# Preparing the feed-forward's first rows some blocks ahead, and multiplying its first chunk in the pause of the local attention's last block

## The chip, the cores and the metric

One core of one Trainium2 chip runs the whole program in one launch. The core has five engines with an instruction queue each: TensorE (PE in the profile, PEld for its weight loads), VectorE (DVE), ScalarE (ACT), GpSimd (POOL) and SyncE (SP), which here only issues DMAs. They meet through semaphores. The metric is the device time of the launch in microseconds; less is better.

## The reference

Four sequences of 1024 rows of 256 numbers go through a layernorm. A causal attention of 16 heads gives `s`; a stack of two layers, each a local attention and a gated feed-forward, gives the gate `g`; the result is `x + s * silu(g)`. The part that matters is one layer:

```python
h = shift_token(x); qkv = h @ wqkv                  # second half of the columns from the row before
q, k = rotary_xpos(l2norm(q) * qs, l2norm(k) * ksc) # 8 heads of 64
x = x + local_attention(q, k, v) @ wo               # window of 128: own block and the one before
h = shift_token(x)
h = (h - h.mean(-1)) / sqrt(h.var(-1) + 1e-5) * lg + lb
a, g = split(h @ w1 + b1, 2)                        # 2 x 682 columns
x = x + (a * gelu(g)) @ w2 + b2
```

## The kernel before, in words

The program runs project, causal attention, and then for each of two layers `phase_window` (local attention) and `phase_feed` (feed-forward). Each phase is a block of its own: all engines meet at its end, and no engine begins the next one before. Every engine's order is written out by hand.

`phase_window` goes over 32 blocks of 128 rows (`NW`; `w` is the block). In step `w` PE runs `project(w+2)` (18 matmuls of 512 columns with the weights `qkv_hi`, `qkv_lo`), `attend(w)` (turn the normalised probabilities `pn` in four parts, turn keys and queries of block `w+1`, then `values`), `turn_h(w+3)`, `score(w+1)` and `output(w)`. DVE runs `normalise(w)` in two halves, `unit(w+1)`, `copy_last`, `cosines` and `sum_squares` of `w+2`, `lo_out`, the `maxima` of `w+1` and `residual(w)`, which writes x1. ACT runs the eight `exps(w)`, which wait for the maxima, and the copies out of PSUM. POOL runs the rotation (`rope`) for `w+2`. SP stores x1 and loads the rows of block `w+4`. A product of full precision is made of three: high by high, high by low, low by high part.

`phase_feed` goes over 8 groups of 512 rows (`SUPERS`; 4 tiles each) and 6 chunks of hidden columns, the last one short. For each chunk PE does `up` (12 matmuls of 512 columns, 6 for the short one) into one of two pairs of PSUM banks (`pH`), ACT does the Gelu and the high part, DVE the product with the gate (`gated`), POOL the low part. A chunk waits for the `gated` of the chunk two before it. In the middle of the first group's chunks PE turns group 1 (`turn(1, 1)`), which needs `hn` of group 1. ACT splits w2 (`w2_hi`, L1627) behind the first chunk's high part.

The attention phase already works for the feed-forward of its layer. SP's `start_feed` in step 28 loads the small constants, w1 (into `qkv_st`, free by then) and, last, two groups of rows. ACT's `feed_weights` makes the high parts of w1 in three parts, the first behind the exps of block 30, two more in step 30; they overwrite `qkv_hi`, so they wait for the last projection. DVE's `feed_split` makes the low parts in steps 30 and 31. For group 0, DVE computes moments at the end of step 30 (`feed_moments`), POOL the deviation, DVE normalises in step 31 (`feed_normalise`), PE turns the rows behind the values of block 31 into banks 0 and 1 of `pS`, the scores' tensor, ACT scales them and makes the high part (`feed_rows`), and DVE makes the low part behind the last residual (`feed_lo`). In step 30 and 31 there is no projection left, so PE has a pause ahead of `attend` (called the pause of block 30 or 31 below).

## Time and profile before

| | us |
|---|---|
| median of 3 runs | 1919.55 (1918.88 to 1920.72) |
| the profiled execution | 1915.72 |
| its span | 1913.6 |
| PE, DVE, ACT, POOL busy | 1816.2, 1462.9, 1211.3, 1000.4 |
| layer 0: attention about 613 to 1047, feed-forward 1047 to 1247 | |
| layer 1: attention 1247 to 1678, feed-forward from 1678 | |

The span is the time from the first to the last instruction of the profiled execution; its time has 2.1 us more around it. PE is busy for 95% of the span, so what counts is where it waits, and at which clock it runs. The busy times of the others say little by themselves: in each stretch one asks what ended the wait of the engine that sets the pace.

### The profile page before, as it was taken

The page shows a single profiled execution, that of the slowest core. Times are in us where ns is not written, and L with a number is a line of the kernel's source. Part 1 is how long each engine was busy: PE and PEld are TensorE (multiplying, and loading weights), DVE is VectorE, ACT ScalarE, POOL GpSimd, SP SyncE. Part 2 cuts the span into 40 slices and gives each one's busy share as a digit, 9 for nine tenths or more (in the row PEclk, how much of TensorE's full clock was granted, in tenths as well). Part 3 has the DMA queues.
Part 4 walks back from the last instruction along what each step waited for, and adds up shares of the span by engine and source line. Part 5 has one row for each costly group of instructions (what it writes and reads, how often), then busy time and mean ns, then how long its engine had stood idle before and what let it go on. Part 6 is the DMA issues. An engine that isn't in the chain of part 4 may idle for free. (4 is left out here: it accounts for less than half of the span.)

```text
span 1913.6 us, 37326 instructions
## 1 busy us (share of the span) xinstructions
PE 1816.2 (95%) x12768; PEld 1298.9 (68%) x12768; DVE 1462.9 (76%) x4115; ACT 1211.3 (63%) x2537; POOL 1000.4 (52%) x807
## 2 busy tenths in 40 slices
PE   7979999999998899999997999989999999889998
PEld 6723333333333788888886888868888888778998
DVE  6678888888882899999997544379999999854543
ACT  4606666666666777777776544358777877655553
POOL 5532223223122778777873444367787778444343
PEclk9959999999999999999998999999999999899999
DMA  8983646455430000100022331100000100242222
GB/s 283 306 145 48 79 57 86 65 73 76 60 48 23 15 29 22 29 29 29 22 58 56 104 114 52 34 30 29 29 24 27 29 29 25 65 126 76 79 78 88
DMA packets 142456, 128.10 MB, mean 67 GB/s; under 512 B 31106, under 2 KB 124734, under 8 KB 142014
## 3 DMA queue, kind: packets, MB, share of 16 engines
q1 hardware_dynamic: 141214, 124.68, 28.4%
q8 instruction: 104, 1.70, 0.4%
q10 hardware_dynamic: 1056, 1.05, 0.2%
q14 instruction: 82, 0.67, 0.1%
HBM read 83.46 MB, written 41.96 MB: 66 GB/s over the span
## 5 line engine op out<-in xcount | busy, mean ns | idle before, releaser
L675 ACT ACTIVATE ca_pr<-ca_pS 128x1024 f32<-128x1024 f32 (+3 forms) x384 | 296.5, 811 | 204.9 <-PE ca_pS L589 163.9
L503 POOL TENSOR_SCALAR_AFFINE_SELECT ca_pr<-ca_pr 128x256 f32<-128x256 f32 x256 | 103.2, 406 | 367.5 <-ACT ca_pr L675 363.1
L704 DVE CUSTOM_DVE_ANT_0 ca_masked<-ca_pR,ca_later 128x256 f32<-128x256 f32 (+3 forms) x512 | 235.6, 485 | 44.7 <-PE ca_pR L565 41.6
L565 PE MATMUL ca_pR<-ca_ks,ca_qs 96*128 96x512 bf16 (+3 forms) x768 | 219.5, 344 | 6.8 <-DVEq L760 3.1
L589 PE MATMUL ca_pS<-ca_qs,ca_ks 98*128 98x512 bf16 (+3 forms) x768 | 183.8, 330 | 12.4 <-issue 6.7
L708 DVE TENSOR_REDUCE ca_mx<-ca_pR 128x1 f32<-128x512 f32 x256 | 175.7, 686 | 25.0 <-PE ca_pR L565 23.2
L565 PEld LDWEIGHTS ca_pR<-ca_ks,ca_qs 96*128 96x128 bf16 x768 | 70.5, 97 | 161.7 <-DVE ca_mx L704 90.1
L941 POOL TENSOR_TENSOR wb_tsn<-wb_qk,base 128x512 f32<-128x512 f32 x62 | 136.5, 2223 | 69.0 <-DVE wb_pn L1156 67.6
L941 POOL TENSOR_TENSOR w_tsn<-w_qk,base 128x512 f32<-128x512 f32 x62 | 136.5, 2222 | 69.0 <-DVE w_pn L1156 67.6
L610 PE MATMUL ca_pO<-ca_pr,ca_va 128*32 128x512 f32 (+3 forms) x1536 | 164.5, 500 | 1.6 <-POOL ca_pr L503 0.8
L1012 ACT ACTIVATE w_pe<-w_sm,w_nmax 128x256 f32<-128x256 f32 (+1 forms) x256 | 123.3, 483 | 67.0 <-DVE w_nmax L1146 66.8
L1012 ACT ACTIVATE wb_pe<-wb_sm,wb_nmax 128x256 f32<-128x256 f32 (+1 forms) x256 | 123.2, 483 | 66.3 <-DVE wb_nmax L1146 66.3
L589 PEld LDWEIGHTS ca_pS<-ca_qs,ca_ks 98*128 98x128 bf16 x768 | 62.2, 98 | 114.5 <-ACT ca_pr L675 66.8
L1156 DVE TENSOR_SCALAR wb_pn<-wb_pe,wb_rsum 128x256 f32<-128x256 f32 (+1 forms) x256 | 97.1, 441 | 2.3
L1156 DVE TENSOR_SCALAR w_pn<-w_pe,w_rsum 128x256 f32<-128x256 f32 (+1 forms) x256 | 96.6, 439 | 2.3
L1146 DVE CUSTOM_DVE_ANT_0 w_sm<-w_pS,masks 128x256 f32<-128x256 f32 (+1 forms) x256 | 88.7, 403 | 9.5 <-PE w_pS L1380 9.3
L1146 DVE CUSTOM_DVE_ANT_0 wb_sm<-wb_pS,masks 128x256 f32<-128x256 f32 (+1 forms) x256 | 88.6, 403 | 9.0 <-PE wb_pS L1380 9.0
L949 POOL TENSOR_TENSOR wb_rs<-wb_ssc,mhalf 128x16 f32<-128x16 f32 x32 | 94.0, 2938 | 2.7
L949 POOL TENSOR_TENSOR w_rs<-w_ssc,mhalf 128x16 f32<-128x16 f32 x32 | 93.9, 2934 | 2.7
L1561 POOL TENSOR_TENSOR f_alo<-f_af,f_ahi 128x512 fp32r<-128x512 f32 x40 | 53.3, 1332 | 54.1 <-ACT f_ahi L1624 54.1
L1561 POOL TENSOR_TENSOR fb_alo<-fb_af,fb_ahi 128x512 fp32r<-128x512 f32 x40 | 53.2, 1330 | 52.9 <-ACT fb_ahi L1624 52.9
L1704 DVE SCALAR_TENSOR_TENSOR fb_af<-fb_pH,fb_b1a,fb_gl 128x512 f32<-128x512 f32 x40 | 30.0, 750 | 63.0 <-ACT fb_gl L1621 58.4
(297 smaller groups left out, 5396.3 us busy)
## 6 DMA issues: line engine op xcount, KB each, us to landing
QKP<-p_parts SPq DMA_DIRECT2D x32, 384.0 KB, 3.6
ca_qs<-QKP SPq DMA_DIRECT2D x96, 128.0 KB, 6.5
ca_ks<-QKP SPq DMA_DIRECT2D x96, 128.0 KB, 7.2
w_xt<-X SPq DMA_DIRECT2D x64, 128.0 KB, 2.2
X<-w_x SPq DMA_DIRECT2D x64, 128.0 KB, 1.7
f_hh<-X SPq DMA_DIRECT2D x32, 256.0 KB, 6.0
X<-p_xn SPq DMA_DIRECT2D x8, 512.0 KB, 4.8
VA<-p_vst SPq DMA_DIRECT2D x8, 512.0 KB, 4.7
```

The source lines that it names most:

```text
L565: pe.matmul(bank[:, 0:w], qs[0:SHIFT_ROW, u, h, i * P:(i + 1) * P], ks[0:SHIFT_ROW, u, h, k0:k0 + w], start=True, stop=True).then_inc(ring ...
L589: ins = pe.matmul(pS[:, pair, hh, 0:w], ks[:, u, h, j * P:(j + 1) * P], qs[:, u, h, q0:q0 + w], start=True, stop=True)
L610: ins = pe.matmul(pO[h * VW:(h + 1) * VW, o:o + w], va[:, u, j, h * VW:(h + 1) * VW], pr[:, k % 2, h // 2, h % 2, 0:w], start=j == 0, stop ...
L675: act.activation(pr[:, k % 2, pair, :, 0:w], pS[:, pair, :, 0:w], ACT.Exp, scale=CS).then_inc(p_ready, 1)
L704: dve.tensor_tensor_reduce(masked[:, jb % RING, 0:w], pR[jb % RING][:, 0:w], later[:, 512 - w:512], -1.0, BIG, ALU.add, ALU.min, mx[:, i, ...
L708: dve.tensor_reduce(mx[:, i, h, ch:ch + 1], pR[jb % RING][:, 0:w], AX.X, ALU.max, negate=True).then_inc(ring_free, 1)
L941: pool.tensor_tensor(*sines(w, j, z), ALU.mult).then_inc(S["ts_ready"], 1)
L949: pool.tensor_tensor(rs[:, j % 2], ssc[:, :], K.mhalf[:, :], ALU.pow).then_inc(S["rs_ready"], 1)
L1012: ins = act.activation(pe_[:, h, 0:keys], sm[:, n, 0:keys], ACT.Exp, bias=nmax[:, n:n + 1], scale=-1.0, accum_out=sums[:, h:h + 1])
L1146: ins = dve.tensor_tensor_reduce(sm[:, n, 0:keys], pS[:, n // 2, n % 2, 0:keys], masks[:, j % 2, 0:keys], -1.0, BIG, ALU.add, ALU.min, nma ...
L1156: ins = dve.tensor_scalar(pn[:, h, 0:keys], pe_[:, h, 0:keys], rsum[:, h:h + 1], None, ALU.mult)
L1561: pool.tensor_tensor(alo[:, j, ch], af[:, ch % 2], ahi[:, j, ch].bitcast(F32), ALU.subtract)\
```

## The change

- SP: `start_feed` runs in step 24 instead of 28, and loads the two groups of rows ahead of the constants and w1.
- DVE: `feed_moments` at the end of step 26 (was 30), `feed_normalise` at the end of step 28 (was inside 31), `feed_lo` at the end of step 30 (was 31). POOL: `feed_deviation` in step 27.
- PE: `feed_turn` ahead of the attend of block 30 (was behind the values of block 31). A new `feed_first` ahead of the attend of block 31 multiplies chunk 0 of group 0 (12 matmuls) into banks 2 and 3 of the scores' tensor, once the maxima of block 31 have been read and the low part is there. The scores of block 31 wait for `feed_rows`.
- ACT: `feed_weights(0)` at the end of step 29, `feed_rows` in its old place behind the exps of block 30, the high part (`feed_high`) in step 30, `feed_weights(1)` and `(2)` behind the copies of step 31. Behind the exps of block 31 a Gelu of one column (`F.warm`).
- The scores' four banks become a tensor shared with the feed-forward (`F.pre`): its first two are `pT`, the other two the first pair of `pH`, so that chunk 0 stands there when the phase starts. `up` begins with chunk 1 for group 0.
- In `phase_feed` DVE normalises group 1 in two halves behind `gated` of chunks 0 and 1 (was ahead of chunk 0).

```diff
@@ SP
-                if w == NW - 4:
+                if w == NW - 8:
                     start_feed()
@@ POOL
+                if w == NW - 5:
+                    feed_deviation()
             steps(step)
-            feed_deviation()
@@ ACT
                 exps(w, j, it, 1)
                 if late == 0:
-                    feed_weights(0)
+                    feed_rows()
+                elif late == 1:
+                    act.activation(F.warm[:, :], F.lng[:, 0:1], ACT.Gelu)
...
                 for ch in range(3):
                     copy_p(w, j, it, ch)
+                if late == 1:
+                    feed_weights(1)
+                    feed_weights(2)
...
                 if late == 0:
-                    feed_weights(1)
-                    feed_weights(2)
+                    feed_high()
                 copy_out(w, j, it)
                 if a3:
                     turned(*a3)
-                if late == 1:
-                    feed_rows()
+                if late == -1:
+                    feed_weights(0)
@@ DVE
-                if late == 1:
-                    feed_normalise()
...
                 residual(w, j, it)
-                if late == 0:
+                if late == -4:
                     feed_moments()
-                elif late == 1:
+                elif late == -2:
+                    feed_normalise()
+                elif late == 0:
                     feed_lo()
@@ PE
+            def feed_first():
+                T = F.sems
+                pe.wait_ge(S["max_ready"], ONE + 2 * (g0 + NW))
+                pe.wait_ge(T["t_lo"], ONE + layer * SUPERS + 1)
+                pe.sem_inc(K.passed, 1)
+                pe.wait_ge(T["w_split"], ONE + 4 * layer + 1)
+                for half in range(2):
+                    cols = slice(half * WHOLE * P, half * WHOLE * P + P)
+                    terms = [(m, t, k) for k in range(KD) for m, t in ((qkv_hi, F.thi), (qkv_hi, F.tlo), (qkv_lo, F.thi))]
+                    for i, (m, t, k) in enumerate(terms):
+                        ins = pe.matmul(feed_bank(2 + half), m[:, k, cols], t[:, k], start=i == 0, stop=i == len(terms) - 1)
+                ins.then_inc(T["g_ready"], 1)
...
                 if a2:
                     project(*a2)
+                if w == NW - 2:
+                    feed_turn()
+                elif w == NW - 1:
+                    feed_first()
                 attend(w, j, it)
@@ phase_feed, DVE
-            for half in range(2):
-                normalise(1, 1, half)
             for ch in range(HC):
                 gated(0, 0, ch)
-                if ch == 2:
+                if ch < 2:
+                    normalise(1, 1, ch)
+                elif ch == 2:
@@ phase_feed, PE
-                for ch in range(HC):
+                for ch in range(0 if s else 1, HC):
```

## Rows read from the trace of the kernel before

**Rows 1.** Windows, block 27: busy us per engine (instructions), granted clock, DMA share, GB/s.

```profile
981.73:994.50 12.77, 12.77 (x106) 10.73 (x105) 11.80 (x33) 9.93 (x28) 9.98 (x6) 1.00 0.09 27
```

**Rows 2.** Timeline of PE, layer 0, blocks 30 and 31 and the feed-forward's start.

```profile
1022.22 1.14 PE L1290 MATMUL w_pX<-ident,w_pn 128*128 128x128 f32 x8 [3.73 <-DVE w_pn L1156]
1023.61 1.94 PE L1290 MATMUL w_pX<-ident,w_pn 128*128 128x128 f32 x8 [0.26 <-DVE w_pn L1156]
...
1036.44 3.39 PE L1290 MATMUL w_pX<-ident,w_pn 128*128 128x128 f32 x16 [4.04 <-DVE w_pn L1156]
1039.76 2.13 PE L1303 MATMUL w_pX<-w_pt,w_v 128*64 128x128 f32 x32
...
1047.27 0.77 PE L1851 MATMUL f_pH<-f_thi,big_hi 128*128 128x512 f32 x1 [2.92 <-PEq L878]
...
1057.15 1.04 PE L1836 MATMUL f_pT<-ident,f_hn 128*128 128x128 f32 x8
```

**Rows 3.** Timeline of DVE over the same stretch.

```profile
1033.21 1.40 DVE L1200 BATCH_NORM_STATS2 f_stt<-f_hh 128x6 f32<-128x256 f32 x4
1034.64 0.38 DVE L1203 BATCH_NORM_AGGREGATE f_mv<-f_stt 128x2 f32<-128x6 f32 x4
...
1037.47 1.38 DVE L1209 TENSOR_SCALAR f_hn<-f_hh,f_mv,f_rstd 128x256 f32<-128x256 f32 x4
...
1044.39 0.42 DVE L1170 TENSOR_TENSOR w_x<-w_pX,w_xt 128x256 f32<-128x256 f32 x1 [1.12 <-PE w_pX L1365]
1045.58 1.22 DVE L1216 TENSOR_TENSOR f_tlo<-f_hf,f_thi 128x1024 fp32r<-128x1024 f32 x1 [0.77 <-ACT f_thi L1075]
...
1055.88 0.75 DVE L1704 SCALAR_TENSOR_TENSOR f_af<-f_pH,f_b1a,f_gl 128x512 f32<-128x512 f32 x1 [2.65 <-ACT f_gl L1621]
```

**Rows 4.** Windows view, PE, of five stretches: PEclk is the granted clock.

```profile
1023.50:1026.50 3.00, 2.89 (x14) 0.50 0.00 0
1047.00:1050.40 3.40, 3.13 (x8) 0.50 0.40 86
1050.63:1056.93 6.30, 6.30 (x29) 1.00 1.12 338
1246.24:1249.00 2.76, 0.63 (x5) 1.00 0.50 163
1717.80:1722.00 4.20, 1.18 (x10) 1.00 0.01 4
```

**Rows 5.** Timeline, DVE, block 27: start us, duration us, engine, line, operation, tiles, count.

```profile
981.94 1.82 DVE L1156 TENSOR_SCALAR w_pn<-w_pe,w_rsum 128x256 f32<-128x256 f32 x4
...
983.91 1.14 DVE L1156 TENSOR_SCALAR w_pn<-w_pe,w_rsum 128x256 f32<-128x256 f32 x4
984.97 1.22 DVE L1135 TENSOR_TENSOR w_qkn<-w_rr,w_rs 128x1024 f32<-128x1024 f32 x1
```

**Rows 6.** Timeline of PE, block 27.

```profile
984.38 1.99 PE L1290 MATMUL w_pX<-ident,w_pn 128*128 128x128 f32 x16
986.29 0.63 PE L1344 MATMUL w_pX<-ident,w_qkn 128*128 128x128 f32 x4
```

**Rows 7.** Timeline of POOL, block 27.

```profile
980.41 2.40 POOL L955 TENSOR_TENSOR w_rr<-w_tc,w_tsn 128x1024 f32<-128x1024 f32 x1
```

**Rows 8.** Timeline of ACT over the same stretch.

```profile
1041.94 0.60 ACT L1022 ACTIVATE w_oth<-w_pX 128x512 fp32r<-128x512 f32 x1 [2.33 <-PE w_pX L1303]
...
1053.79 1.47 ACT L1627 ACTIVATE f_w_hi<-f_w_st 128x1536 fp32r<-128x1536 f32 x1
```

**Rows 9.** Timeline of ACT: a table load ahead of a Gelu.

```profile
1748.67 1.28 ACT L1666 ACT_TABLE_LOAD   x1
1749.97 0.20 ACT L1666 ACTIVATE fb_junk<-fb_lng 128x1 f32<-128x1 f32 x1
```

**Rows 10.** Timeline of PE at the start of layer 1's attention.

```profile
1247.69 0.30 PE L1259 MATMUL wb_pX<-ident,w_xt 128*128 128x128 f32 x1 [1.45 <-PEq L1447]
```

**Rows 11.** Windows view, ACT, start of feed-forward; last column GB/s.

```profile
1047.08:1052.00 4.92, 1.53 (x2) 0.66 0.62 178
```

More of the change, by code:

```diff
@@ L908, in start_feed @@
                 sp.sem_inc(K.passed, 1)
+                for i in range(2):
+                    sp.wait_ge(S["x1_stored"][i], ONE + (layer * (NW // 2) + SUP) * 16)
+                sp.sem_inc(K.passed, 1)
+                for i in range(2):
+                    load_h(sp, F, layer, X, i, i)
                 feed_constants()
@@ L915, in start_feed @@
                           .then_inc(F.sems["w1_loaded"], 16)
-                for i in range(2):
-                    sp.wait_ge(S["x1_stored"][i], ONE + (layer * (NW // 2) + SUP) * 16)
-                sp.sem_inc(K.passed, 1)
-                for i in range(2):
-                    load_h(sp, F, layer, X, i, i)
             def step(w, j, it):
-                if w == NW - 4:
+                if w == NW - 8:
                     start_feed()
@@ L1073, in feed_rows, with feed_high @@
                     ins.then_inc(T["hf_ready"], 1)
+            def feed_high():
+                T = F.sems
                 act.wait_ge(T["hf_ready"], ONE + KD * (layer * SUPERS + 1))
@@ L1329, in attend, with feed_turn @@
                     values(w, j, it, ch)
-                if w == NW - 1:
-                    pe.wait_ge(S["max_ready"], ONE + 2 * (g0 + NW))
-                    pe.wait_ge(F.sems["hn_ready"], ONE + layer * SUPERS + 1)
-                    for k in range(KD):
-                        for n in range(SUP):
-                            ins = pe.transpose(feed_bank(k)[:, n * P:(n + 1) * P], F.hn[:, n, k * P:(k + 1) * P],
-                                               K.ident[:, :])
-                    ins.then_inc(F.sems["t_ready"], 1)
+            def feed_turn():
+                pe.wait_ge(S["max_ready"], ONE + 2 * (g0 + NW - 1))
+                pe.wait_ge(F.sems["hn_ready"], ONE + layer * SUPERS + 1)
+                for k in range(KD):
+                    for n in range(SUP):
+                        ins = pe.transpose(feed_bank(k)[:, n * P:(n + 1) * P], F.hn[:, n, k * P:(k + 1) * P],
+                                           K.ident[:, :])
+                ins.then_inc(F.sems["t_ready"], 1)
+            def feed_first():
+                T = F.sems
+                pe.wait_ge(S["max_ready"], ONE + 2 * (g0 + NW))
[8 more added lines that the diff above has]
+                ins.then_inc(T["g_ready"], 1)
             def turn_k(w, j, it):
@@ L1372, in score @@
                     pe.wait_ge(S["qt_copied"], ONE + 1 + g0 + w + 1)
+                    if w == NW - 1:
+                        pe.wait_ge(F.sems["hf_ready"], ONE + KD * (layer * SUPERS + 1))
                 if w > 0:
@@ L1431, in phase_feed @@
     res = [w2_st[:, KD:KD + SUP], xr[:, 0]]
-    ao_bank = lambda s, z: pT[:, z] if s < L - 1 else pH[:, s - L + 1, z]
+    ao_bank = lambda s, z: pT[:, z] if s < L - 1 else pH[s - L + 1][:, z]
     last = lambda s: int(s == L)
@@ L1620, in gelus @@
                     rows = slice(0, P) if ch < WHOLE else slice(GATE_ROW, GATE_ROW + TAIL)
-                    act.activation(gl[rows, ch % 2], pH[rows, ch % 2, 1], ACT.Gelu, bias=b1g[rows, ch:ch + 1])\
+                    act.activation(gl[rows, ch % 2], pH[ch % 2][rows, 1], ACT.Gelu, bias=b1g[rows, ch:ch + 1])\
                        .then_inc(S["gelu_done"], 1)
@@ L1703, in gated @@
                 if ch < WHOLE:
-                    dve.scalar_tensor_tensor(af[:, ch % 2], pH[:, ch % 2, 0], b1a[:, ch:ch + 1], gl[:, ch % 2],
+                    dve.scalar_tensor_tensor(af[:, ch % 2], pH[ch % 2][:, 0], b1a[:, ch:ch + 1], gl[:, ch % 2],
                                              ALU.add, ALU.mult).then_inc(S["act_ready"], 1)
@@ L1708, in gated @@
                     for row0 in (0, GATE_ROW):
-                        ins = dve.scalar_tensor_tensor(af[row0:row0 + TAIL, ch % 2], pH[0:TAIL, ch % 2, 1],
+                        ins = dve.scalar_tensor_tensor(af[row0:row0 + TAIL, ch % 2], pH[ch % 2][0:TAIL, 1],
                                                        b1a[rows, ch:ch + 1], gl[rows, ch % 2], ALU.add, ALU.mult)
@@ L1850, in up @@
                         for i, (m, t, k) in enumerate(terms):
-                            ins = pe.matmul(pH[:, ch % 2, half], m[:, k, cols], t[j][:, k], start=i == 0,
+                            ins = pe.matmul(pH[ch % 2][:, half], m[:, k, cols], t[j][:, k], start=i == 0,
                                             stop=i == len(terms) - 1)
@@ L1938, with window_tensors @@
     pass
-def window_tensors(nc, c, W):
+def window_tensors(nc, c, W, F):
     sb = lambda n, s, d: c.enter_context(nc.sbuf_tensor(W.name + n, s, d))
@@ L1955, in window_tensors @@
         sb("oth", [P, INNER], F32R), sb("otl", [P, INNER], F32R), W.x1,
-        ps("pX", [P, 4, 512], F32), ps("pS", [P, 4, 2, 2 * P], F32))
+        ps("pX", [P, 4, 512], F32), F.pre[:, :, :].rearrange("p b (s t) -> p b s t", s=2))
 def shared_tensors(nc, c, F):
@@ L1965, in shared_tensors @@
     F.ve, F.rstd = sb("ve", [P, 2, SUP], F32), sb("rstd", [P, 2, SUP], F32)
+    F.pre = c.enter_context(nc.psum_tensor(F.name + "pre", [P, 4, N], F32))
+    F.warm = sb("warm", [P, 1], F32)
     F.hn, F.hf = sb("hn0", [P, SUP, D], F32), sb("hf", [P, KD, N], F32)
@@ L1981, in feed_tensors @@
         sb("xb", [P, 2, SUP, D], F32), F.x2,
-        ps("pT", [P, KD, N], F32), ps("pH", [P, 2, 2, N], F32), ps("pO", [P, 2, 512], F32))
+        F.pre[:, 0:KD], [F.pre[:, KD:4], ps("pH", [P, 2, N], F32)], ps("pO", [P, 2, 512], F32))
     O = F.closing
@@ L2060, in program @@
                 with ExitStack() as cw:
-                    window_tensors(nc, cw, W)
+                    window_tensors(nc, cw, W, F)
                     phase_window(nc, K, W, F, layer, X, wqkv, wo, qk_scales, w1, ln_g, ln_b, b1)
```

## The prediction, as it was made before the changed kernel ran

> **What bounds the kernel now.** I read the busy shares by slice first: PE is busy at nine tenths nearly everywhere, so a change is worth what it takes from PE's waits and from its stretches at the lower clock. Then the windows view of a single attention block, then the timelines of PE, DVE and ACT around the seam between attention and feed-forward in layer 0. Layer 1 has the same seam, so each sum is made once and doubled.
>
> In an undisturbed block PE is busy for all of its 12.77 us; DVE has 11.80 of work in it [rows 1]. The step is PE's, with DVE close behind. At the seam three things cost PE time. Ahead of the turns of blocks 30 and 31 it stands 3.73 and 4.04 us, since no projection fills the time in which DVE and ACT make the probabilities [rows 2]. Between the last output and the feed-forward's first matmul it stands 2.92 us [rows 2], while DVE finishes `feed_lo`: last residual 1044.39, `feed_lo` 1045.58 for 1.22 [rows 3]. And behind each such pause it runs at 1.2 instead of 2.4 GHz for a while: granted clock 0.50 from 1023.5 to 1026.5 and from 1047.0 to 1050.4 [rows 4].
>
> **Part 1: work moved into blocks 26 to 29.** `feed_moments` is 1.40 plus 0.38 us of DVE; it ended block 30 and now ends block 26. `feed_normalise` is 1.38 us [rows 3], now at the end of block 28. Both push the next block's normalise back. What that costs follows from the chain to `turn_k`: the unit vectors are ready at 984.97 + 1.22 = 986.19, PE turns them at 986.29 [rows 5, 6], so there is 0.1 of slack. But the first half of the normalise takes 1.82 beside POOL's addition, which runs until 982.81, and the second half 1.14 without it [rows 5, 7]. Pushed back by 1.4 or more, both halves run alone, which gives 0.68 back. So the moments cost 1.73 (the two overlap a little) - 0.68 - 0.1 = 0.95, the normalise 1.38 - 0.68 - 0.1 = 0.6: together **1.6 us lost per layer**. PE has no idle time in later blocks out of which it could win this back [rows 1]. The bounds are 0 (all of it in DVE's 0.97 us of idle per block, two blocks) and 3.1 (both in full). I take 1.6, because the chain above ends at a PE that is full.
>
> Free are: the deviation, on POOL behind its rotation (only a DVE step two blocks later waits for it); SP's fourteen issues four blocks earlier (w1, the constants, the rows), which end before that block's x1 is ready, and behind which only that store and the rows four blocks ahead are queued; ACT's first weight copy at the end of block 29, in the time in which it waits for the maxima; and PE's eight transposes in block 30's pause. If SP's issues did run over, `turn_h` one block later would be the first to feel it.
>
> **Part 2: the pause of block 30.** The eight transposes now break it in two. The two turn groups behind it took 1.14 + 1.94 = 3.08 us there, at the low clock, against 1.99 in an undisturbed block [rows 2, 6]. Does the clock now stay? The nearest row is the seam between the layers: 0.63 us of PE work in 2.76 us, in small pieces, and the clock stays at 1.00 [rows 4]. The pause with its transposes (about 1.0 in 3.7, half of sixteen in 1.99 [rows 6]) looks like that, so I take it as kept: **1.1 us won per layer**; the bounds are 0 and 1.1, and this is close to even. ACT's `feed_rows` stands where a weight copy of the same length stood; the new wait of the scores on it is met five us early.
>
> **Part 3: the pause of block 31.** `feed_lo` (1.22) now starts behind block 30's residual, in place of the moments at 1033.21, so the low part is there at 1034.43 [rows 3]. Chunk 0 is 12 matmuls. At the full clock a step is 0.233 us (29 matmuls in 6.30 us, 27 steps) [rows 4], so it fills 1034.5 to 1037.35. Behind it PE turns the probabilities (ready by then) in 1.99 us [rows 6] and starts on the values at 1039.35; before, that was 1039.76 [rows 2]: 0.4 us earlier, although PE turned up 0.9 later, since before the turns took 3.39 at the low clock. The values, the output and the residual behind them keep their lengths: the transposes taken out there ran beside ACT's copy at 1041.94 [rows 8], which released the output, and so save nothing. ACT's two weight copies fit in the 2.33 us it waited there [rows 8].
>
> The Gelu of one column brings the table load ahead: 1.28 us, and the next activation begins at once, for 0.20 [rows 9]. The exps end by 1036.1, since the second half of the normalise (0.2 + 1.14) [rows 5] comes between them and 1037.47 [rows 3]; load and Gelu end by 1037.6, and the first copy is due at 1037.35 + 0.5, so they are free. The Trainium skill ("ScalarE: Activation LUTs", What ACT_TABLE_LOAD costs) charges a drain of 1.38 us more for each switch. By that rule the copy would come 0.5 us late and the sum would lose 0.5 per layer; the row shows no such drain behind the load.
>
> **Part 4: the seam.** With `feed_lo` gone the seam is ended by the residual and SP's store. The other seam, which also ends so, leaves PE idle for 1.45 us [rows 10] instead of 2.92: 1.5 won, and the clock stays up. With the 0.4 of part 3 the feed-forward starts **1.9 us earlier per layer**, at 1045.4.
>
> **Part 5: inside the feed-forward.** PE starts with chunk 1, so it is 12 matmuls ahead, which took 8 x 0.43 and 4 x 0.23 = 4.4 us with the low clock [rows 4]. Most of it isn't kept. `turn(1, 1)` needs `hn` of group 1, whose second half now stands behind `gated` of chunk 1, and that is behind ACT's Gelu of chunk 1, and that is behind `w2_hi`, which waits for w2's DMA. The DMA is issued at the phase's start and isn't moved with the chunk. When does it land? By 1052.0 the queue has moved 4.92 us x 178 GB/s = 876 KB [rows 11], and b2 and w2 are 852 KB of 1024 bytes (872 KB of 1000): no earlier than 4.7 us after PE's start (1047.27). ACT began `w2_hi` at 1053.79 without waiting [rows 8]: no later than 6.5. I take 5.6, the middle. From `w2_hi` to the end of `gated` of chunk 1 it was 1055.88 + 0.75 - 1053.79 = 2.84 [rows 3, 8]; half of a normalise (0.7) and a signal (0.1) make 3.65. So `turn(1, 1)` comes 9.25 us after PE's start. Before it was 1057.15 - 1047.27 = 9.88 [rows 2]: only 0.6 won. And PE stands from 5.65 (two chunks) to 9.25, 3.6 us, so it falls to the low clock as behind 3.73. A stretch at that clock costs half of its 3.4 us or 8 x 0.2 [rows 4]: 1.6. Part 5 is **1.0 lost per layer**; bounds +1.5 (early DMA, clock kept) and -1.9.
>
> The Trainium skill ("DMA: Bandwidth & Descriptors", Anatomy of one DMA) puts about 2 us of fixed cost on a transfer, most of it the receipt behind the last byte. By that rule w2 would land at the late bound and part 5 would lose 0.9 more per layer; the trace shows only the two bounds.
>
> **Sum.** -1.6 + 1.1 + 1.9 - 1.0 = 0.4 us won per layer, 0.8 in both. The profiled execution took 1915.72 (span 1913.6), 3.8 below the median of the runs; its sum would be 1914.9, and against the median of 1919.55 it is 1918.7. I call differences under 0.2% (3.8 us) no change, about what a measurement of this kernel can tell.
>
> **The rivals.**
> - *The clock holds behind the feed-forward's wait too* (faster). For it: PE stood 3.02 us at 1718 and came back at clock 1.00 [rows 4]. Against it: the gaps of 2.92, 3.73 and 4.04 were each followed by the low clock [rows 2, 4]. Part 5 is then +0.6: 2.0 per layer, 4.0 in all, 1915.5. With DVE's work hidden as well it would be 1912.3. Chance 0.25.
> - *The clock falls in both pauses, under chunk 0* (slower). The pause of block 31 still starts with 2.1 us of nothing. If the clock falls while chunk 0 runs, chunk 0 and the turns take up to 1.7 longer, all on PE's path, and part 2's 1.1 is gone: 0.4 - 2.8 = -2.4 per layer, 1924.3. [...] Against it: PE is dense from 1034.5 on. Chance 0.15.
> - *Only block 30's pause stays slow*: -0.7 per layer, 1920.9. For it: 1.0 us of transposes is little. Chance 0.22.
> - *The chunk only moves PE's wait* (the change doesn't do what it says): w2 lands at the late bound, PE waits 4.5 us for `turn(1, 1)`, part 5 is -1.9: 1920.5. Chance 0.08.
> - The forecast as summed: 0.30.
>
> **Chances and range.** Faster than 1915.7: most of the first rival and a little of the forecast with DVE's work hidden, 0.27. Slower than 1923.4: the second rival and a bit of the others with DVE's work in full, 0.16. Within: 0.57. The range goes from the first rival with its bound, 1912.3, to the second, 1924.3.
>
> **What would show it.** PE's gap ahead of the feed-forward near 1.45 us (part 4). Clock 1.00 behind block 30's pause (part 2), and chunk 0's matmuls 0.233 apart (part 3). PE idle about 3.6 us ahead of `turn(1, 1)`, released by DVE's `hn`, with ACT idle ahead of `w2_hi` (part 5): were that wait absent, part 5 would be wrong by up to 4 us per layer, and the kernel clearly faster. Blocks 27 and 29 longer than 12.77 by 0.95 and 0.6 (part 1): were they unchanged, 3.2 us more would be won in all.

## The result

| | us |
|---|---|
| before, median of 20 runs | 1919.31 (1914.76 to 1923.19) |
| after, median of 20 runs | 1923.05 (1920.33 to 1928.14) |
| ratio of after to before | 1.0027, 95% interval 1.0019 to 1.0035 |
| profiled execution of after, its span | 1921.14, 1919.1 (before 1915.72, 1913.6) |
| PE, DVE, ACT, POOL busy, after | 1817.5, 1464.0, 1213.2, 1001.5 |

The change made the kernel slower by 0.27%, 5.2 us; the forecast was 0.8 us faster. (The two medians lie 3.7 us apart; the ratio and its interval are what is used below.) The direction was wrong. The time lies inside the range given, near its slow end, where the second rival (1924.3) was priced. The mechanism is another one: the third and the fourth rival came true together, each of which had been priced alone, and the clock fell at one more place.

I first set the starts of each block's residual (DVE `w_x`) and of each `gated` in after against before, so that a gain or a loss is seen in the block where it arises. Then I read the places that the forecast named. PE's timeline of layer 0 in the kernel after (start, duration, engine, line, output and inputs, count, idle time ahead and who ended it), to be set beside [rows 2]:

```profile
1020.94 1.09 PE L1343 MATMUL f_pre<-ident,f_hn 128*128 128x128 f32 x8 [0.62 <-DVE w_nmax L1153]
1024.14 1.06 PE L1297 MATMUL w_pX<-ident,w_pn 128*128 128x128 f32 x8 [2.11 <-DVE w_pn L1163]
1025.40 1.94 PE L1297 MATMUL w_pX<-ident,w_pn 128*128 128x128 f32 x8 [0.20 <-DVE w_pn L1163]
...
1036.53 0.47 PE L1357 MATMUL f_pre<-f_thi,big_hi 128*128 128x512 f32 x1 [2.13 <-DVE f_tlo L1223]
1036.83 0.39 PE L1357 MATMUL f_pre<-f_tlo,big_hi 128*128 128x512 f32 x1
...
1039.39 1.94 PE L1297 MATMUL w_pX<-ident,w_pn 128*128 128x128 f32 x16
...
1047.04 0.47 PE L1878 MATMUL f_pH<-f_thi,big_hi 128*128 128x512 f32 x1 [1.40 <-PEq L878]
...
1057.04 1.94 PE L1863 MATMUL f_pre<-ident,f_hn 128*128 128x128 f32 x8 [4.17 <-issue]
1058.63 0.77 PE L1878 MATMUL f_pH<-f_thi,big_hi 128*128 128x512 f32 x1
1059.20 0.63 PE L1878 MATMUL f_pH<-f_tlo,big_hi 128*128 128x512 f32 x1
```

The reader sees the eight transposes in block 30's pause and 1.94 for eight more behind it, which is the low clock; chunk 0 at the full clock in block 31's pause (1036.53 to 1039.39); the seam at 1.40 instead of 2.92; and then a wait of 4.17 us ahead of `turn(1, 1)`, with the low clock behind it. PE's granted clock by windows, kernel after (stretch, length, PE busy and count, clock, DMA share and GB/s):

```profile
1025.00:1028.00 3.00, 2.80 (x15) 0.55 0.00 0
...
1036.50:1046.00 9.50, 8.41 (x72) 1.00 0.01 2
...
1056.00:1062.50 6.50, 5.46 (x17) 0.50 0.43 115
```

Who holds `turn(1, 1)` is on ACT and DVE. First ACT, then DVE, kernel after:

```profile
1049.48 0.63 ACT L1651 ACTIVATE f_ahi<-f_af 128x512 fp32r<-128x512 f32 x1 [1.87 <-DVE f_af L1731]
1053.45 1.48 ACT L1654 ACTIVATE f_w_hi<-f_w_st 128x1536 fp32r<-128x1536 f32 x1 [3.34 <-DMA f_w_st<-w]
1054.84 0.67 ACT L1648 ACTIVATE f_gl<-f_pH,f_b1g 128x512 f32<-128x512 f32 x1
```
```profile
1055.55 0.75 DVE L1731 SCALAR_TENSOR_TENSOR f_af<-f_pH,f_b1a,f_gl 128x512 f32<-128x512 f32 x1 [3.45 <-ACT f_gl L1648]
1056.21 0.72 DVE L1717 TENSOR_SCALAR f_hn<-f_hh,f_mv,f_rstd 128x256 f32<-128x256 f32 x2
```

Read from the second row on: w2's DMA releases ACT's `w2_hi` at 1053.45, 6.41 us after PE's start; behind it come the Gelu of chunk 1, `gated`, the second half of the normalise, and PE at 1057.04. "issue" in PE's row is only the profile's word for a wait it could not name.

The drift (after minus before) by part, in us; minus is a gain:

| | forecast, per layer | layer 0 | layer 1 |
|---|---|---|---|
| block 27 (moments) | 0.95 | 0.80 | 0.80 |
| block 29 (normalise) | 0.6 | 0.94 | 1.30 |
| block 30 | -1.1 | 0.50 | 0.53 |
| block 31 | -0.4 | -0.71 | -0.76 |
| seam | -1.5 | -1.51 | -1.52 |
| inside the feed-forward | 1.0 | 2.8 | 1.16 |
| wait ahead of layer 1's first down projection | 0 | | 1.46 |
| sum | -0.4 | 2.8 | 3.0 |

With -0.3 from ahead of all this, 2.8 + 3.0 - 0.3 = 5.5 is the whole difference of the two spans.

### The profile page after: what moved, and what is told of

It reads as the page before. It is cut to its first block and busy times, and to the rows that moved or that the text cites. A ratio compares the mean times of both kernels' runs of the same rounds, so it can differ in the third digit from the quotient of the medians.

```text
span 1919.1 us, 37332 instructions
## 1 busy us (share of the span) xinstructions
PE 1817.5 (95%) x12768; PEld 1296.8 (68%) x12768; DVE 1464.0 (76%) x4115; ACT 1213.2 (63%) x2539; POOL 1001.5 (52%) x807
## 3 DMA queue, kind: packets, MB, share of 16 engines
q10 hardware_dynamic: 1056, 1.05, 0.2%
## 5 line engine op out<-in xcount | busy, mean ns | idle before, releaser
L1153 DVE CUSTOM_DVE_ANT_0 w_sm<-f_pre,masks 128x256 f32<-128x256 f32 (+1 forms) x256 | 88.6, 403 | 9.6 <-PE f_pre L1403 9.6
L1153 DVE CUSTOM_DVE_ANT_0 wb_sm<-fb_pre,masks 128x256 f32<-128x256 f32 (+1 forms) x256 | 88.5, 403 | 9.0 <-PE fb_pre L1403 9.0
L1288 PE MATMUL w_pX<-big_hi,w_thi 128*128 128x512 f32 x192 | 77.1, 402 | 0.7 <-DVE w_tlo L1122 0.7
```

The lines of the kernel that those rows point to most:

```text
L1153: ins = dve.tensor_tensor_reduce(sm[:, n, 0:keys], pS[:, n // 2, n % 2, 0:keys], masks[:, j % 2, 0:keys], -1.0, BIG, ALU.add, ALU.min, nma ...
```

## The experiments

All ratios are to the kernel before, run on the same chip; "us" is the ratio times 1917, the median of before in these series (1916.3 to 1917.9). x1 to x4, x5 to x8 and x9 to x14 ran on three different chips, each with the kernel before beside it, so across these groups only ratios are compared. The difference of two rows has an interval of 2.2 to 3.7 us to either side, which is why the lengths of the blocks in the traces are set beside the smaller ones.

| run | ratio, 95% interval | us |
|---|---|---|
| the changed kernel | 1.0027 (1.0019 to 1.0035) | +5.2 |
| x1_w2_late | 0.9994 (0.9985 to 1.0002) | -1.2 |
| x2_filler | 1.0008 (1.0000 to 1.0017) | +1.5 |
| x3_rows_early | 1.0032 (1.0021 to 1.0043) | +6.1 |
| x4_no_first | 1.0011 (1.0001 to 1.0020) | +2.1 |
| x5_w2_mid | 0.9968 (0.9956 to 0.9979) | -6.1 |
| x6_mid_fill | 0.9948 (0.9936 to 0.9960) | -10.0 |
| x7_act_norm | 0.9911 (0.9896 to 0.9926) | -17.1 |
| x8_all | 0.9884 (0.9871 to 0.9897) | -22.2 |
| x9_mid_shift | 0.9935 (0.9920 to 0.9949) | -12.5 |
| x10_norm_noshift | 0.9945 (0.9929 to 0.9960) | -10.5 |
| x11_before_shift | 0.9976 (0.9967 to 0.9986) | -4.6 |
| x12_after_noshift | 1.0026 (1.0015 to 1.0036) | +5.0 |
| x13_mid_no_first | 0.9987 (0.9976 to 0.9998) | -2.5 |
| x14_before_mid | 1.0010 (1.0000 to 1.0020) | +1.9 |

Two theories stood behind the first runs. Theory A: the wait on w2 and the low clock behind it eat the seam's gain, on top of a part 1 that costs more than summed. Theory B, the rival: the loss is all in the blocks ahead, and the wait only stands where PE would have waited anyway.

### w2's split moved to the end of the group

```diff
-                    if s == 0 and ch == 0:                 # ACT, behind chunk's high part
+                    if s == 0 and ch == HC - 1:            # ACT, between Gelu and high part
                         act.wait_ge(S["w_loaded"], ONE + (layer + 1) * 4 * 16)
                         act.activation(w2_hi[:, :, :], w2_st[:, :, :], ACT.Copy).then_inc(S["w_hi"], 1)
...
-                elif ch == 2:                              # DVE, w2_lo
+                elif ch == HC - 1:
```

> The changed kernel with w2's split taken from behind chunk 1 to behind chunk 5 of the first group (ACT's high part and DVE's low part), so that nothing ahead of turn(1, 1) waits for w2's DMA. Theory A (the new wait on w2 and the low clock behind it eat the gain of the seam): turn(1, 1) starts within 6 us of PE's first matmul of the feed-forward instead of 10.0, the 4.17 us gap of layer 0 and the 3.86 us gap of layer 1 are gone, the clock stays at 1.00 from 1047 to 1063; the feed-forward gets 4 to 6.5 us shorter in layer 0 and 3 to 5 in layer 1, and the kernel comes out 7 to 11 us below the changed one, 1912 to 1916, that is faster than the kernel before. Theory B (PE's wait goes elsewhere, to the wait ahead of the down projection for w2's low part, or the loss is all in blocks 26 to 29): under 2 us below the changed kernel, 1921 to 1923.

6.3 us less than the changed kernel (0.33%), just short of theory A's 7 to 11; the rival's 2 us are out. `turn(1, 1)` came 6.5 us after PE's start (1047.48 to 1053.96; 6 or less was expected), with 0.66 us of wait instead of 4.17, and the clock stayed at 1.00. But about 2 us per layer went to a new wait. DVE, POOL and PE of this run, in this order:

```profile
1065.56 3.96 DVE L1830 TENSOR_TENSOR f_w_lo<-f_w_st,f_w_hi 128x1536 fp32r<-128x1536 f32 x1
```
```profile
1065.51 2.40 POOL L1582 TENSOR_TENSOR f_xb<-f_xr,f_b2t 128x1024 f32<-128x1024 f32 x1
```
```profile
1070.24 0.50 PE L1878 MATMUL f_pre<-f_thi,big_hi 128*128 128x512 f32 x1 [1.59 <-DVE f_af L1731]
```

w2's low part took 3.96 us where it took 1.75 before the move: POOL's step had begun 0.05 earlier, and 1065.51 + 2.40 + 1.75 = 1069.66 is 0.14 from where it ended. The time is that of a DVE which did nothing until POOL was through. The Trainium skill ("SBUF — State Buffer", SBUF: two separate sides) says that the port pair which the two share is an exclusive lock and the later one blocks fully; this row agrees.

### The clock held up across the wait

```diff
                 pe.wait_ge(S["w_split"], ONE + 4 * layer + 3)
+                for i in range(14):
+                    pe.matmul(pO[:, 1], w1_hi[:, 0, 0:P], thi[0][:, 0], start=True, stop=True)
                 turn(1, 1)
```

> The changed kernel with fourteen extra matmuls of 512 columns (about 3.3 us at full clock) ahead of turn(1, 1), whose result nothing reads: the wait on w2 stays, only the clock is held up across it. If the low clock behind the gap costs what it seems to in the trace (matmuls 0.43 apart for 5 to 6.5 us in layer 0, 0.50 for 3.8 us in layer 1): turn(1, 1) still starts about 10 us after PE's start, the clock stays at 1.00 behind it, and the kernel is 3 to 5 us below the changed one, 1918 to 1920. If the length of the wait alone matters, it is equal to the changed kernel within 1 us. If the clock holds in neither or falls in both, no change as well: the granted clock from 1056 to 1063 tells which.

3.6 us less than the changed kernel, within the 3 to 5 expected. PE's rows, and the clock behind the wait (0.50 in the changed kernel):

```profile
1053.67 3.43 PE L1932 MATMUL f_pO<-f_thi,big_hi 128*128 128x512 f32 x14
1057.82 1.09 PE L1863 MATMUL f_pre<-ident,f_hn 128*128 128x128 f32 x8 [0.71 <-DVE f_hn L1717]
```
```profile
1057.20:1063.60 6.40, 5.78 (x29) 1.00 0.37 99
```

`turn(1, 1)` still comes 9.8 us after PE's start, so the wait is untouched: 3.6 us of the loss are the low clock behind it, in both layers together. By the starts of residual and `gated` in the trace, 2.8 of it came back in layer 0 and 1.3 in layer 1. `w2_hi` began 6.26 us after PE's start here.

### Part 1 alone

The kernel before, with the rows loaded at block 24 and the deviation behind block 27's rotation; the transposes, `feed_lo` and chunk 0 stay late.

```diff
-                if late == 1:                              # ahead of block 31's unit
-                    feed_normalise()
...
-                if late == 0:
+                if late == -4:
                     feed_moments()
+                elif late == -2:
+                    feed_normalise()
```

> The kernel before with part 1 alone: the rows are loaded four blocks earlier, the moments end block 26, the deviation ends block 27 on POOL, the normalise ends block 28 on DVE; transposes, low part and chunk 0 stay where they were. If DVE's steps cost what the trace of the changed kernel suggests (0.8 for the moments, 0.94 and 1.3 for the normalise beside POOL's addition), blocks 27 and 29 lengthen by 1.7 to 2.1 us per layer together, blocks 30 and 31 get back 0 to 1.2 from the moments and the normalise that they lose, and the kernel is 1 to 4 us slower than before: 1920.5 to 1923.5. If DVE's steps are hidden by its idle time, it is 0 to 2.4 us faster: 1917 to 1919.5.

6.1 us slower, more than any theory said (1 to 4). The blocks of the profiled run account for 4.0: blocks 27 and 29 are 0.81 and 1.00 longer in layer 0 and 0.80 and 1.30 in layer 1, block 30 0.50 and 0.11 longer, block 31 0.12 and 0.37 shorter, so 2.2 and 1.8. It gives back less than I thought, although the moments no longer stand behind block 30. In this run 1.9 more lie at the seam between the layers, which part 1 does not touch (last section). So part 1 costs about 4 by the blocks; the 6.1 of the runs has 2 us of interval.

Why the normalise costs more than its 1.38 [rows 3] is in the changed kernel's DVE and POOL rows:

```profile
1007.36 0.42 DVE L1177 TENSOR_TENSOR w_x<-w_pX,w_xt 128x256 f32<-128x256 f32 x1
1007.70 2.34 DVE L1216 TENSOR_SCALAR f_hn<-f_hh,f_mv,f_rstd 128x256 f32<-128x256 f32 x4
```
```profile
1006.51 2.41 POOL L954 TENSOR_TENSOR w_rr<-w_tc,w_tsn 128x1024 f32<-128x1024 f32 x1
```

It starts 1.22 us before POOL's addition ends, and takes 2.34 us, not 1.38. The 0.68 us that the probabilities win by standing later are paid, as 0.96, by the step put in front of them. The sum of 1.38 and 1.22 would be 2.60, so here the meeting cost 0.26 less than all of POOL's rest.

### The changed kernel without the chunk

```diff
-                elif w == NW - 1:
-                    feed_first()
...
-                for ch in range(0 if s else 1, HC):
+                for ch in range(HC):
```

> The changed kernel without chunk 0 in block 31's pause: its twelve matmuls, Gelu and high part are done in the feed-forward as before, all other moves stay. Theory A (the chunk moves PE's wait to w2's DMA): the pause of block 31 is about 4 us again with the low clock behind it (0.7 to 1.1 us lost per layer), the seam stays near 1.4 us, turn(1, 1) starts within 9 us of PE's start with chunk 0 and 1 and 2 ahead of it, so the feed-forward's own time from start to end is back within 1 us of that of the kernel before; in sum equal to the changed kernel within 2 us. If the chunk is a clear gain, it is over 3 us slower than the changed kernel; if it is the harm itself, over 3 us faster.

3.1 us less than the changed kernel: outside theory A's 2 us, at the border of "the harm itself". Without the chunk in the pause PE has one more chunk to multiply ahead of `turn(1, 1)`: there it waits 1.75 and 1.29 us in the two layers instead of 4.17 and 3.86, and the clock stays at 1.00 behind it. The transfer of w2 still ends this wait (`turn(1, 1)` came 10.4 and 9.9 us after PE's start, not within 9), which the kernel before did not have: there the phase began at the low clock [rows 4] and came to `turn(1, 1)` at 9.9 us without a wait, since its matmuls took that long. So in the kernel as changed the chunk costs more than it brings; the difference of 3.1 us has an interval of 2.4.

### w2's split at chunk 2

```diff
-                    if s == 0 and ch == 0:
+                    if s == 0 and ch == 2:                 # ACT, between Gelu and high part
```

DVE's low part stays as in the changed kernel, behind `gated` of chunk 2.

> The changed kernel with w2's high part on ACT between the Gelu and the high part of chunk 2 of the first group, where ACT stood 0.82 us in the run with the late split, and w2's low part on DVE where the change has it, in a gap that was 3.71 us there. Theory A (all that the late split still lost is that DVE's low part took 3.96 us beside POOL at a busy time, and PE waited 0.25, 0.25 and 1.59 us for it): those waits are gone, no new wait ahead of turn(1, 1), 2 us less per layer than with the late split, 3 to 5 us in all, so 1911 to 1914, 3 to 6 us below the kernel before. Rival (the w2 split costs ACT or DVE its length wherever it stands): within 1.5 us of the late split, and a wait of 1 us or more appears ahead of turn(1, 1) or of chunk 5.

11.3 us less than the changed kernel and 6.1 less than the kernel before, at the upper end. ACT's and DVE's rows of this run:

```profile
1054.87 0.67 ACT L1648 ACTIVATE f_gl<-f_pre,f_b1g 128x512 f32<-128x512 f32 x1
1055.44 1.48 ACT L1652 ACTIVATE f_w_hi<-f_w_st 128x1536 fp32r<-128x1536 f32 x1
1056.81 0.62 ACT L1654 ACTIVATE f_ahi<-f_af 128x512 fp32r<-128x512 f32 x1
```
```profile
1056.95 1.76 DVE L1830 TENSOR_TENSOR f_w_lo<-f_w_st,f_w_hi 128x1536 fp32r<-128x1536 f32 x1 [0.62 <-ACT f_w_hi L1652]
1060.48 0.75 DVE L1731 SCALAR_TENSOR_TENSOR f_af<-f_pH,f_b1a,f_gl 128x512 f32<-128x512 f32 x1 [1.77 <-ACT f_gl L1648]
```

`w2_hi` finds its data there, and the low part keeps its 1.76 us and ends 1.77 before the next `gated`. This time DVE was first and POOL paid: its low part of chunk 2, 1.29 us one chunk before, took 2.35, and 1058.71 (the end of DVE's step) + 1.29 = 1060.00 is 0.14 from where it ended.

```profile
1055.04 1.29 POOL L1588 TENSOR_TENSOR f_alo<-f_af,f_ahi 128x512 fp32r<-128x512 f32 x1 [1.87 <-ACT f_ahi L1654]
1057.51 2.35 POOL L1588 TENSOR_TENSOR f_alo<-f_af,f_ahi 128x512 fp32r<-128x512 f32 x1 [1.18 <-ACT f_ahi L1654]
```

Of PE's waits inside the group only 0.66, 0.29 and 0.25 are left. Inside the feed-forward this run gains 3.3 and 3.5 us on the kernel before, where the changed one lost 2.8 and 1.16.

### The two pauses filled

To the run above, in the pauses of blocks 30 (behind the transposes) and 31 (ahead of chunk 0):

```diff
+            def filler(w):
+                pe.wait_ge(S["kt_copied"], ONE + 1 + g0 + w + 1)
+                for i in range(8):
+                    pe.matmul(pX[:, 1], wo_hi[:, 0, 0:P], wo_hi[:, 0:2].rearrange("p k n -> p (k n)"), start=True,
+                              stop=True)
```

> As the run with the split at chunk 2, with eight extra matmuls of 512 columns (1.9 us at full clock, result overwritten) in the pause of block 30 behind the transposes of the feed-forward's rows, and eight in the pause of block 31 ahead of chunk 0, where PE stood 2.1 us each. It tells what the clock costs in the two pauses. If the low clock in them is set by what PE does in the pause: clock 1.00 from 1020 to 1046 and in layer 1 alike, block 30 takes 12.7 instead of 14.1 us and block 31 10.8 in the same run, 1.0 to 1.6 us less per layer, 2 to 3 in all against the split at chunk 2. If the clock falls for another reason: it falls with the filler as well, and the time is the same within 1 us. If the filler itself delays the transposes of the probabilities: slower by up to 1 us.

3.8 us less than without them, a little over the 2 to 3; the blocks below account for 1.5 in layer 0 and 2.0 in layer 1. Windows of the run with the fillers, then of the one without, over blocks 30 and 31 of layer 0 and 1:

```profile
1019.00:1032.00 13.00, 11.88 (x104) 1.00 0.03 11
1032.00:1046.00 14.00, 11.61 (x87) 1.00 0.07 24
1648.00:1662.00 14.00, 13.02 (x107) 1.00 0.05 16
1662.00:1674.00 12.00, 9.78 (x78) 1.00 0.06 20
```
```profile
1022.00:1035.00 13.00, 9.74 (x92) 1.00 0.04 12
1035.00:1048.00 13.00, 9.96 (x72) 0.87 0.03 10
1650.00:1664.00 14.00, 11.60 (x91) 0.76 0.03 9
1664.00:1677.00 13.00, 8.76 (x74) 1.00 0.06 20
```

With them the clock is at 1.00 in all four, and block 30 takes 12.72 and 13.04, block 31 10.80 in both. Without them one of the two pauses is followed by the low clock in each layer, but not the same one: block 31 in layer 0 (12.35), block 30 in layer 1 (15.06). In the changed kernel it was block 30 both times. The transposes alone do not keep the clock; whether it falls behind them or only under chunk 0 differs between the profiled kernels and between the layers: in layer 0 x1 and x5 have block 30 at 12.69 and block 31 at 12.36 and 12.35 (with the clock kept it is 10.80), so there block 30 did get shorter (it was 13.58 before), and block 31 lost it again.

### Part 1 made cheap, and all together

x5 with the moments in two halves, behind blocks 25 and 26, and the normalise on ACT behind block 28; its bias, `-mean * rstd`, is made by two small POOL steps and kept in a new tensor `F.nb`. x8_all has the fillers too.

```diff
+                for n in range(SUP):                       # ACT, late == -2
+                    ins = act.activation(F.hn[:, n], F.hh[:, 0, n], ACT.Identity, bias=F.nb[:, 1, n:n + 1],
+                                         scale=F.rstd[:, 0, n:n + 1])
...
+                if late in (-5, -4):                       # DVE, two of the four bn_stats each
+                    feed_moments(late + 5)
```

> As the run with the split at chunk 2, with part 1's DVE work made cheap: the four moments in two halves, at the ends of blocks 25 and 26, and the normalise on ACT in four Identity steps at the end of block 28, where ACT waits 2.2 us for the maxima. If part 1's cost is DVE's time in the chain to the transposes of the unit vectors: blocks 27 and 29 are back from 13.57 and 13.45 to within 0.4 us of 12.77 and 12.5, block 26 is longer by 0.1 to 0.3, and the kernel 2.5 to 4 us below the split at chunk 2. If it is something else that the early rows bring (their loads, POOL's deviation, a shared port): blocks 27 and 29 stay over 0.6 longer each and the gain is under 1 us.

> Both of the last two together: w2's split at chunk 2, moments halved and normalise on ACT, and the fillers in both pauses. If the three causes (w2's wait, DVE's work in blocks 26 to 29, the clock in the pauses) are separate, the gains add: 9 to 13 us below the changed kernel, 1907 to 1911 where the kernel before takes 1917. If they cover one another, it is within 1.5 us of the better of the two.

The first gained 10.9 us where 2.5 to 4 were expected, so something more than part 1's cost was in it. The blocks did what was said: 27 takes 12.92 instead of 13.57 and 29 12.08 instead of 13.44, and ACT's step (2.07 us) fits its wait for the maxima with 0.26 to spare:

```profile
1001.30 2.07 ACT L1074 ACTIVATE f_hn<-f_hh,f_nb,f_rstd 128x256 f32<-128x256 f32 x4
1003.63 0.51 ACT L1016 ACTIVATE w_pe<-w_sm,w_nmax 128x256 f32<-128x256 f32 x1 [0.26 <-DVE w_nmax L1167]
```

But all other blocks were at 12.77 too, not 12.83, and each group of the feed-forward 0.4 shorter. The new tensor moves every tensor allocated behind it by 32 bytes per partition, which makes 64 against the kernel before, since the change's own `F.warm` had moved them by 32. Four runs separate this.

### Where the tensors lie

x9 is x5 with `F.nb` allocated and unused; x10 is x7 with the values in a free slot of `F.ve`, so nothing moves; x11 is the kernel before with 64 unused bytes ahead of `hn0`; x12 is the changed kernel without its own `F.warm` (4 bytes, which moved the tensors behind it by 32).

```diff
+    F.nb = sb("nb", [P, 2, SUP], F32)                      # x9, ahead of F.warm and hn0
...
+    F.pad = sb("pad", [P, 16], F32)                        # x11, ahead of hn0
...
-    F.warm = sb("warm", [P, 1], F32)                       # x12
```

> The run with the split at chunk 2 plus a tensor of 32 bytes per partition that nothing uses, allocated where the run with the normalise on ACT has its new one. That run was 10.7 us faster than the split at chunk 2, of which blocks 26 to 29 show 3.9; the rest is spread over the whole kernel (blocks of 12.77 instead of 12.83 us from the first on, 0.4 us per group of the feed-forward, matmuls of 512 columns 0.228 instead of 0.233 apart in parts of a projection). If that rest comes from where the tensors behind the new one lie: 5 to 8 us faster than the split at chunk 2, blocks at 12.77. If it comes from anything else in that run: equal to the split at chunk 2 within 1 us, blocks at 12.83.

> The run with the normalise on ACT and the halved moments, with the new values kept in a slot of an existing tensor, so that all tensors lie as in the changed kernel. If part 1's work costs what the blocks show: 3 to 5 us faster than the split at chunk 2 (1911.2 beside a kernel before of 1917.9), blocks 27 and 29 at 12.9 and 12.1 to 12.5, the other blocks at 12.83. If placement is not the matter: 10 to 11 us faster, blocks at 12.77.

> The kernel before with 64 bytes per partition that nothing uses ahead of the feed-forward's tensors, the same shift as in the run with the normalise on ACT. If placement is what gave that run its rest: 4 to 7 us faster than the kernel before, and blocks at 12.77. Otherwise equal within 1.5 us.

> The changed kernel without its own new tensor of four bytes (the Gelu of one column writes into a free slot instead), so that all tensors lie as in the kernel before. If the change's own shift of 32 bytes is part of its loss: 1 us or more faster than the changed kernel. The drift of the blocks in the trace (0.06 longer in three or four of 26 blocks, the feed-forward 0.1 shorter) says 0.3 us in all, so equal within 1 us, 0.2 to 0.3% above the kernel before.

x9 is 6.3 us faster than x5, with nothing but the shift, and its blocks are at 12.77. x10 is 4.4 faster than x5, with its blocks at 12.83 and only 27 and 29 short (12.91 and 12.14): so 4.4, with an interval of 3.7, is what part 1's DVE work cost; in its trace blocks 27 and 29 are 1.95 shorter in either layer than in x5, and block 26 is 0.35 longer in layer 1, where the halved moments stand. The kernel before wins 4.6 when its tensors are moved to the same place. x12 is equal to the changed kernel within the interval of 2.5: no loss from the shift of 32 bytes that the change brought by itself can be seen. PE's matmuls of 512 columns, grouped by line (count, busy, mean ns of one), in x5 and then in x9:

```profile
L1288 PE MATMUL w_pX<-big_hi,w_tlo 128*128 128x512 f32 x192 | 76.7, 400 | 0.0
L1878 PE MATMUL f_pH<-f_tlo,big_hi 128*128 128x512 f32 x80 | 31.6, 395 | 0.0
```
```profile
L1288 PE MATMUL w_pX<-big_hi,w_tlo 128*128 128x512 f32 x192 | 76.0, 396 | 0.0
L1878 PE MATMUL f_pH<-f_tlo,big_hi 128*128 128x512 f32 x80 | 31.2, 390 | 0.0
```

The same instructions take 4 to 5 ns less each, and they follow one another faster: ten steps within the chunks take 2.33 us in x5 (1072.62 to 1074.95) and 2.27 in x9 (1071.99 to 1074.26). Over some 2000 such pairs the mean step is 0.228 us in x7, x9 and x11, whose tensors lie 64 bytes behind their place in the kernel before, and 0.233 in the kernel before, x12 (both 0), the changed kernel, x5 and x10 (all 32). Which operand's address does it, and why, stays open: by the sizes of the allocations `thi0` lies at 64 modulo 128 in the fast ones, at 0 and at 32 in the others, but all its neighbours moved with it.

x8_all came out at 1895.3, 27.4 below the changed kernel, where 9 to 13 had been expected: 11.3 (w2's split) + 3.8 (fillers) + 4.4 (part 1) + 6.3 (shift) = 25.8. Within their intervals the causes add. Against the kernel before with the same shift (x11) it is ahead by 17.6 us.

### What the chunk is worth

x13 is x5 without chunk 0 in the pause; x14 is the kernel before with the split at chunk 2.

> The run with the split at chunk 2, without chunk 0 in block 31's pause (its twelve matmuls, Gelu and high part in the feed-forward). It tells what the chunk is worth once nothing waits for w2 ahead of turn(1, 1). If the chunk's 2.8 us of matmuls were only cancelled by that wait: 2.5 to 3.5 us lost per layer against the split at chunk 2, 5 to 7 in all, that is level with the kernel before within 2 us. If the chunk is worth little in any case: within 2.5 us of the split at chunk 2, 3 us or more below the kernel before.

> The kernel before with only w2's high part moved on ACT to between the Gelu and the high part of chunk 2. If the wait on w2 was made by the change (in the kernel before ACT began w2's high part without waiting, and PE stood 0.26 us ahead of turn(1, 1)): within 1 us of the kernel before. If the earlier place cost the kernel before as well: 2 us or more faster.

x13 is 3.6 us slower than x5, between the two expectations: with w2's split moved the chunk is worth 1.8 us per layer, though it takes 2.8 us of matmuls out of the feed-forward (the 3.6 has an interval of 3.1; the spans of the two profiled runs differ by 2.2). x14 is 1.9 slower than the kernel before, at the edge of its interval and outside both expectations: the old place of the split was no cost there. The change made it one, by taking away the chunk, and with the clock now kept at the seam also the slow start, that had covered w2's transfer.

## Why the prediction was wrong

The step that failed first is part 2: the clock was taken as kept behind the transposes, for 1.1 us won per layer, and it fell, for 0.5 lost. The second is part 5, with the right chain and two terms too small in layer 0: the landing of w2 and the low clock behind PE's wait. Term by term:

**Part 1** had the right mechanism (the DVE chain to the transposes of the unit vectors; block 27 +0.80 for 0.95). The term for the normalise was mis-sized: 0.94 and 1.30 for 0.6, since I gave it its undisturbed 1.38 us and let only the step behind it feel POOL. In all 1.74 and 2.10 for 1.6, and the blocks behind it did not give the moments' time back. (The 1.73 of the sum for the moments is a little short too: from the start of the one step to the end of the other [rows 3] has 1.81.)

**Part 2** failed, and with its sign. I took the clock as kept behind the transposes, from a row in which PE did little and kept it [rows 4]. It fell, and block 30 became 0.5 longer instead of 1.1 shorter: the clock stayed as slow as before, and the normalise of the probabilities took 2.13 us instead of 1.71, because it now runs beside POOL's addition for 1.19 us (1021.86 to 1023.05) instead of 0.77 (1020.36 to 1021.13). 1.6 us missed per layer, the largest error together with part 5. The row I leaned on does not even hold for itself: the seam of [rows 4] is followed by the low clock in five of the sixteen profiled runs (below).

**Part 3** held: the chunk in the pause, 0.233 per step, at the full clock, the table load and the two weight copies free (1.28 us of load at 1037.68, 0.20 of Gelu at 1038.97, the first copy at 1040.03 after 0.85 of idle time). -0.71 and -0.76 for -0.4. The drain of 1.38 that the Trainium skill ("ScalarE: Activation LUTs", What ACT_TABLE_LOAD costs) charges for a switch is not in this trace either: load and Gelu start 1.29 apart, and the load starts 0.02 behind the last exp's read-out (1037.66).

**Part 4** held to 0.02 us: 1.51 and 1.52 for 1.5.

**Part 5** named the chain and mis-sized two of its terms. w2's split began 6.41 us after PE's start, not 5.6: close to the late bound of 6.5. The rest of the chain held (3.59 us for 3.65), so `turn(1, 1)` came at 10.0, not 9.25. The Trainium skill ("DMA: Bandwidth & Descriptors", Anatomy of one DMA) has a fixed cost of about 2 us per transfer, stated there for transfers that GpSimd issues, while here SP issues them. In this trace the queue had moved 4.50 us x 198 GB/s = 891 KB by 1052.0, which is as much as b2 and w2 (872 KB), and `w2_hi` began 1.45 us later, so the cost behind the last byte is near 1.5 us if the queue moved them in the order of issue (ACT's windows view of the kernel after, last column GB/s):

```profile
1047.50:1052.00 4.50, 0.74 (x2) 1.00 0.67 198
```

And the low clock behind the wait lasted from 1056 to 1062.5 in layer 0 and cost 2.8 us there and 1.3 in layer 1 by the trace of x2 (3.6 in both by its runs), where I had 1.6 in each. Layer 1 lost 1.16, near the 1.0; layer 0 2.8, beyond the bound of 1.9. I had this case as a rival of its own at 0.08 with 1920.5; but it stood alone there, with part 2 still won. Together with the third rival it would have read 0.4 - 1.1 - 0.9 = -1.6 per layer, 1922.8. Of the terms that missed, part 2's had been taken at its good bound and the other two in the middle of theirs.

**Another 1.46** came at a place that I had read, as a row for a rival, and put at nothing in the sum: PE waits 3.02 us ahead of layer 1's first down projection in both kernels; the clock held in the profiled run of before [rows 4] and fell in that of after. It fell in thirteen of the sixteen profiled runs and held in before, x3 and x6 alone, so the row I had read was the rare case, and this part of the difference of the two profiles is luck and no effect of the change that could be shown.

In sum 1.6 + 1.8 (layer 0) and 1.6 + 0.2 + 1.5 (layer 1) from parts 2 and 5 and this wait, 0.1 and 0.5 from part 1, less 0.3 per layer from part 3, make 6.7 less 0.3 from ahead of it all: 6.4, against 5.5 + 0.8 = 6.3 missed in the profile. The runs bear out the three causes: 4.4 for part 1 (x10), 3.8 for the clock in the pauses (x6), and 11.3 for the wait on w2 with its clock (x5). The last is more than the 4.0 that the feed-forward lost in the table, because with the wait gone the work saved by the chunk counts as well.

## What to carry to other kernels

When a piece of work is taken out of the head of a phase, ask which transfer of that phase it was covering, and move the first step that waits for that transfer back by as much; here one wait in the wrong place turned 6.1 us of gain into 5.2 of loss. A DVE step that starts while POOL is in one of its long steps can cost nearly its own time plus what is left of POOL's (2.34 for 1.38 with 1.22 left, 3.96 for 1.75 with 2.35 left), so price a moved step from a row in which the two meet. A clock that stayed up in one profile is one sample; take its price from several. And before a small gain is put down to an edit, check that the edit moved no tensor: an unused allocation was worth as much as the edit itself.

## What I had not expected of the hardware

**The clock after the same wait differs from one profiled run to the next.** The seam between the layers is the same code with the same wait of 1.44 or 1.45 us in nearly all of the sixteen kernels profiled; the clock behind it stayed at 1.00 in eleven profiled runs and fell in five. These are different kernels, each profiled once; but the kernel before by itself, on one chip in the series of x13, took 1914.3 us at a mean clock of 0.978 and 1921.7 at 0.974. The run with the late split, against 1.45 and clock 1.00 in [rows 10, 4]:

```profile
1246.49 0.30 PE L1266 MATMUL wb_pX<-ident,w_xt 128*128 128x128 f32 x1 [1.44 <-PEq L1474]
```
```profile
1247.00:1250.60 3.60, 2.88 (x9) 0.66 0.80 239
```

When it falls it costs 1.6 to 1.9 us: across the seam the drift goes from -1.2 to +0.4 in x1, from 3.2 to 5.1 in x3 and from -6.25 to -4.3 in x6. So a term that rests on the clock being kept behind one such wait has a chance, not a value, and a profile of one run can be off by that much: x3's span was 6.9 above before's, its runs 6.1.

**A shift of the tensors** to 64 bytes behind their place in the kernel before was worth 4.6 to 6.3 us, 0.24 to 0.33%, as much as all that was at stake in the change; the first 32 of these bytes did nothing that could be measured (x12).
